# Edge-weight sums of the build: GpSimd compares only, TensorE weighs the hits and keeps a diagonal

## What is computed

```python
src, dst, edge_weight1      # 200000 edges, sorted by dst
h = relu(layernorm(x)); x = x + agg(h)                       # layer 0: degree-normed sums over edges
h = relu(layernorm(x)); x = x + gat2(h)                      # layer 1: two attention layers
h = relu(layernorm(x)); x = x + gat(h)                       # layer 2: attention
h = relu(layernorm(x)); x = x + message_mlp(h, edge_weight1) # layer 3

def _mp_layer(x, src, dst, edge_attr, W, b):                 # twice in layer 3
    msg = concat([x[dst], x[src], edge_attr], 1) @ W + b
    return relu(segment_sum(msg, dst, n))
```

## Time and profile before

| | us |
|---|---|
| runs (3) | 3001.86, 3004.49, 3005.86 |
| median | 3004.49 |
| profiled execution, span | 2998.9 |
| DVE busy in the span | 2360.0 (79%) |
| PE busy | 2558.4 (85%) |
| ACT busy | 1602.9 (53%) |
| POOL busy | 564.6 (19%) |

### The profile page before, as it was taken

One profiled execution on the slowest core, in us unless ns is written; L12 is line 12 of the kernel. 1 busy time (PEld: TensorE's weight loads), 2 busy tenths in 40 slices (PEclk: granted clock), 3 DMA queues, 4 the chain that ended last, 5 costly groups with the idle time before them and its releaser, 6 DMA issues. The chain is left out here.

```text
span 2998.9 us, 77361 instructions
## 1 busy us (share of the span) xinstructions
PE 2558.4 (85%) x25762; PEld 2119.5 (71%) x25763; DVE 2360.0 (79%) x5456; ACT 1602.9 (53%) x2016; POOL 564.6 (19%) x1356
## 2 busy tenths in 40 slices
PE   3648998999899968999878888759999967999998
PEld 2635555555555548999857687639999957888997
DVE  8979999999999976666699999979999995222212
ACT  6023444344444439999898788659888841000101
POOL 0007666676666600000000000000000000000000
PEclk9879999999999988999989899879999978999999
DMA  3003443343344245676536555415545616888998
GB/s 101 0 1 94 113 114 81 99 130 89 81 118 120 80 162 173 221 252 220 188 109 215 171 171 173 149 65 173 185 164 188 214 64 236 293 291 299 322 365 300
DMA packets 448144, 493.82 MB, mean 165 GB/s; under 512 B 132101, under 2 KB 447465, under 8 KB 447850
## 3 DMA queue, kind: packets, MB, share of 16 engines
q1 hardware_dynamic: 300920, 409.16, 40.9%
q10 hardware_dynamic: 147060, 82.71, 9.4%
HBM read 402.61 MB, written 89.17 MB: 164 GB/s over the span
## 5 line engine op out<-in xcount | busy, mean ns | idle before, releaser
L2595 PE MATMUL psum<-sb_arena 128*128 128x198 bf16 (+2 forms) x14406 | 1115.8, 239 | 150.6 <-DVE sb_arena L1883 90.6
L2595 PEld LDWEIGHTS psum<-sb_arena 128*128 128x128 f16 x14406 | 1048.1, 99 | 218.1 <-DVE sb_arena L1883 138.5
L3212 ACT ACTIVATE sb_arena<-sb_arena 128x896 f16 (+1 forms) x1029 | 1014.8, 1047 | 159.1 <-PE psum L2595 123.8
L1877 DVE TENSOR_TENSOR sb_arena<-sb_arena 128x896 f16<-128x896 f16 x1029 | 635.1, 621 | 140.1 <-ACT sb_arena L3212 118.4
L1176 DVE TENSOR_SCALAR sb_arena<-sb_arena 128x392 f16<-128x392 f16 x2352 | 664.6, 348 | 0.0
L2874 ACT ACTIVATE sb_arena<-psum 128x784 f16<-128x784 f32 x392 | 323.2, 824 | 469.1 <-PE psum L2243 404.0
L2243 PE MATMUL psum<-sb_arena 128*128 128x392 f16 x2352 | 479.4, 340 | 79.0 <-DVE sb_arena L1176 65.4
L2243 PEld LDWEIGHTS psum<-sb_arena 128*128 128x128 bf16 x2352 | 280.2, 128 | 257.3 <-DVE sb_arena L1176 103.4
L2660 PE MATMUL psum<-sb_arena 128*128 128x192 bf16 x4802 | 413.8, 247 | 28.9 <-DVEq L2008 16.1
L2660 PEld LDWEIGHTS psum<-sb_arena 128*128 128x128 f16 x4802 | 402.5, 98 | 39.2 <-DVEq L2008 16.9
L1883 DVE TENSOR_TENSOR sb_arena<-sb_arena 128x896 f16<-128x896 f16 x686 | 423.1, 617 | 0.0
(11 more groups left out here) (380 smaller groups left out, 1468.7 us busy)
## 6 DMA issues: line engine op xcount, KB each, us to landing
sb_arena<-counts SPq DMA_DIRECT2D x245, 896.0 KB, 6.6
sb_arena<-counts SPq DMA_DIRECT2D x245, 672.0 KB, 4.7
counts<-sb_arena ACTq DMA_DIRECT2D x56, 1344.0 KB, 5.6
sb_arena<-records SPq DMA_DIRECT2D x392, 6.0 KB, 1.7
sb_arena<-records ACTq DMA_DIRECT2D x392, 6.0 KB, 1.7
counts<-sb_arena SPq DMA_DIRECT2D x1, 5488.0 KB, 19.0
records<-sb_arena SPq DMA_DIRECT2D x1, 3124.0 KB, 8.9
counts<-sb_arena ACTq DMA_DIRECT2D x14, 112.0 KB, 1.7
```

The source lines that it names most:

```text
L1877: nc.vector.tensor_tensor(above_at[r % RING], above_at[r % RING], counts_of(g, j), ALU.mult).then_inc(above_ready, 1)
L2595: last = nc.tensor.matmul(psum[:, bank, at:at + wide], of[:, b * BLK:(b + 1) * BLK], moves[side][:, r, :], start=(r == 0 and at == 0), sto ...
L3212: nc.scalar.activation(above_at[r % RING], of, ACT.Sigmoid, bias=steep_s[:, r:r + 1], scale=STEEP).then_inc(signs_ready, 1)
```

## The change

GpSimd keeps the subtraction and the comparison of each group of four windows; its multiplication and its two additions go. The hits go into one of four buffers (HITS = 4), ordered by tile, so that the 64 hits of one tile lie together. TensorE takes them as weights, with eight moving columns: the edge weights of the group's eight half windows in that tile. Three such matmuls, one for each tile, accumulate a block of 64 rows and 8 columns, of which only the diagonal in steps of 8 rows is wanted. PSUM keeps 56 columns for a chunk instead of 7, ScalarE copies 56, and VectorE masks them at the end with `ea_own`, which it makes once, and adds up each 8.

The matmuls come at the end of the group's last window, behind the pairs, and wait for that group's own hits, no longer for those of the group before. ScalarE's copy moves from window 3 to window 0 of the even half, ahead of the copies of layer 0's sums. `LEA` becomes a buffer of its own, and the buffers behind `ea_hit` lie 640 bytes further on.

```diff
+        def edge_hits_of(i):
+
+            hit = ea_hit[:, i % HITS, :].rearrange("p (t k d) -> p t k d", t=ST, d=SUB)
+            at = at_dst.rearrange("p w (g d) -> p (w g) d", d=SUB).unsqueeze(1).broadcast_to([BLK, ST, 2 * EG, SUB])
+            dst_rel = rel[:, i * EG:(i + 1) * EG, :].rearrange("p w (g t c) -> p t (w g) c", t=ST, c=3)[:, :, :, 1]
+            return hit, at, dst_rel.unsqueeze(3).broadcast_to([BLK, ST, 2 * EG, SUB])
+
...
-                nc.gpsimd.iota(at_dst[:], [[0, 2 * ST], [1, SUB]], base=0, channel_multiplier=0, allow_small_or_imprecise_dtypes=True)
-                pool.drain()
-                nc.gpsimd.tensor_scalar(at_dst[:, ST:2 * ST, :], at_dst[:, ST:2 * ST, :], float(SUB), None, ALU.add)
-                nc.gpsimd.memset(ea_win[:, WH // EG - 1, :], 0.0)
+                nc.gpsimd.iota(at_dst[:], [[0, EG], [1, WIN]], base=0, channel_multiplier=0, allow_small_or_imprecise_dtypes=True)
+                for p0 in (0, EG * WIN):
+                    pool.drain()
+                    nc.gpsimd.iota(ea_past[p0:p0 + EG * WIN, :], [[-SUB, 2 * EG]], base=0, channel_multiplier=1, allow_small_or_imprecise_dtypes=True)
                 pool.drain().then_inc(ea_ready, 1)
                 pool.sem_inc(rel_ready, WS)
...
-                        edge_sums(h, k // EG)
-
-                def edge_sums(h, i):
-
-                    n = WH // EG
-                    wins = rel[:, i % n * EG:(i % n + 1) * EG, :].rearrange("p w (t c) -> p w t c", c=3)
-                    hit = ea_hit.rearrange("p (w t) d -> p w t d", w=EG)
-                    thirds = ea_hit.rearrange("p (w t) d -> p w t d", t=ST)
-                    to = ea_win[:, i % n, :].rearrange("p (w d) -> p w d", d=SUB)
+                        edge_hits(h, k % WH // EG, k // WH)
+
+                def edge_hits(h, i, later):
+
+                    hit, at, dst_rel = edge_hits_of(i)
                     pool.drain()
-                    pool.wait_ge(ea_used, h * n + (i + 1))
-                    nc.gpsimd.tensor_tensor(hit, at_dst[:].unsqueeze(1).broadcast_to([BLK, EG, 2 * ST, SUB]),
-                                            wins[:, :, :, 1].unsqueeze(3).broadcast_to([BLK, EG, 2 * ST, SUB]), ALU.subtract)
+                    pool.wait_ge(ea_used, h * (WH // EG) + (later * (WH // EG) + i + 1))
+                    nc.gpsimd.tensor_tensor(hit, at, dst_rel, ALU.subtract)
                     pool.drain()
-                    nc.gpsimd.tensor_scalar(ea_hit[:], ea_hit[:], 0.0, None, ALU.is_equal)
-                    pool.drain()
-                    nc.gpsimd.tensor_tensor(hit, hit, wins[:, :, :, 2].unsqueeze(3).broadcast_to([BLK, EG, 2 * ST, SUB]), ALU.mult)
-                    pool.drain()
-                    nc.gpsimd.tensor_tensor(to, thirds[:, :, 0, :], thirds[:, :, 1, :], ALU.add)
-                    pool.drain()
-                    nc.gpsimd.tensor_tensor(to, to, thirds[:, :, 2, :], ALU.add).then_inc(ea_ready, 1)
+                    nc.gpsimd.tensor_scalar(ea_hit[:, i % HITS, :], ea_hit[:, i % HITS, :], 0.0, None, ALU.is_equal).then_inc(ea_ready, 1)
 
...
+                dve.wait_ge(ea_ready, 1)
+                nc.vector.tensor_scalar(ea_own[:], ea_past[:], 0.0, None, ALU.is_ge)
+                dve.drain()
+                nc.vector.scalar_tensor_tensor(ea_own[:], ea_past[:], float(SUB), ea_own[:], ALU.is_lt, ALU.mult)
...
-                nc.vector.tensor_copy(ea_sum[:], LEA[:, CB:(CHUNKS + 1) * CB])
+                nc.vector.tensor_tensor(LEA[:, CB:(CHUNKS + 1) * CB, :], LEA[:, CB:(CHUNKS + 1) * CB, :],
+                                        ea_own[:].unsqueeze(1).broadcast_to([BLK, NB, 2 * EG]), ALU.mult)
+                dve.drain()
+                nc.vector.tensor_reduce(ea_sum[:], LEA[:, CB:(CHUNKS + 1) * CB, :], AX.X, ALU.add)
...
-                pe.sem_inc(ea_used, 6)
+                pe.sem_inc(ea_used, HITS - 1)
...
-                def edge_sum(slot, i):
-
-                    odd, n = 1 - slot, WH // EG
-                    p0 = (odd + i) % 2 * EG * WIN
-                    at = EA_AT + (n * odd + i) // 2 % CB
-                    nc.tensor.matmul(psum[p0:p0 + EG * WIN, 5, at:at + 1], ea_win[:, i % n, :], ones[:, 0:1], start=True, stop=True).then_inc(ea_used, 1)
+                def edge_sum(odd, i, h):
+
+                    g = odd * (WH // EG) + i
+                    p0, at = g % 2 * EG * WIN, g // 2 * 2 * EG
+                    wins = rel[:, i * EG:(i + 1) * EG, :].rearrange("p w (g t c) -> p (w g) t c", t=ST, c=3)
+                    pe.wait_ge(ea_ready, h * (WH // EG) + (i + 2))
+                    for t in range(ST):
+                        last = nc.tensor.matmul(psum[p0:p0 + EG * WIN, 5, at:at + 2 * EG], ea_hit[:, i % HITS, t * EG * WIN:(t + 1) * EG * WIN], wins[:, :, t, 2],
+                                                start=t == 0, stop=t == ST - 1, skip_group_check=True)
+                    last.then_inc(ea_used, 1)
 
                 def behind(slot, k, n, c, h):
 
-                    adds = k % EG == EG - 1 and (k < EG or not isinstance(h, int))
-                    if adds:
-                        pe.wait_ge(ea_ready, h * (WH // EG) + (k // EG + 1))
-                    if adds:
-                        edge_sum(slot, k // EG - 1)
...
                             behind(1 - odd, k, w, c, h)
+                            if k % EG == EG - 1:
+                                edge_sum(odd, k // EG, h)
...
-                    act.wait_ge(ea_used, h * (WH // EG) + 7)
-                    to = LEA[:, bass.ds(c * CB, CB)] if not isinstance(c, int) else LEA[:, c * CB:(c + 1) * CB]
-                    nc.scalar.copy(to, psum[:, 5, EA_AT:EA_AT + CB])
+                    act.wait_ge(ea_used, h * (WH // EG) + (HITS - 1))
+                    to = LEA[:, bass.ds(c * CB, CB), :] if not isinstance(c, int) else LEA[:, c * CB:(c + 1) * CB, :]
+                    nc.scalar.copy(to.rearrange("p b k -> p (b k)"), psum[:, 5, 0:CB * 2 * EG])
...
+                            if odd == 0 and k == 0:
+                                edge_sums_out(c, h)
                             if k == 0:
                                 half_sums(odd, h)
-                            if odd == 0 and k == EG - 1:
-                                edge_sums_out(c, h)
```

23 lines of the change are left out of this document (12 added, 11 removed).

## The result

In the same rounds the changed kernel takes 2975.1 us in the median (2967.1 to 2981.6), the kernel before 3003.2 (2999.6 to 3005.9): the ratio is 0.9906, with an interval of 0.9891 to 0.9922. That is 28.1 us less, where 34.5 were forecast; the time lies 5 us above the forecast of 2970 and within its range. Timed a second time with later experiments, the change had 2976.4 (2966.6 to 2986.1), ratio 0.9909 (0.9889 to 0.9930). Its runs lie further apart than those of before, and that turns out to be a part of the story.

What follows compares the result with a forecast made beforehand. VectorE was taken to bound the kernel. Chunks falling from 117.2 to 112.1 us gain 33, the first half 2.8, less 1.1 at the end: 34.7. 3004.5 less 34.5 gives 2970.0 us, range 2960 to 2990.

Steps and rivals of the forecast that it cites:

- VectorE bounds, and loses to GpSimd: Build windows: VectorE sets the pace, 2.093 us a window over a floor of 1.86, losing 0.93 a group to GpSimd's work.
- The term: VectorE in the build: removing GpSimd's three instructions gives back 0.40 us a group, so 111.6 us a chunk.
- the fit: Least squares of 391 VectorE window distances on GpSimd's time in each line: its three instructions cost 0.41 us a group.
- Two more matmuls at 0.27: TensorE at each group's end: two more matmuls cost 0.27 us, in 12 places a chunk, 3.2 us.
- dear matmuls: Rival: two more matmuls cost 0.45 to 0.6 us and TensorE becomes the bound, 2982 to 2994 us; chance 0.17.
- accumulation that doesn't overlap: Rival: matmuls accumulating into the same columns cost full duration, 0.88 us for two; 3016 us, slower than before; chance 0.05.
- TensorE's sum: TensorE's chunk without waits for VectorE: 108.5 us, plus 3.2 for new matmuls and 0.2 for ScalarE's copy, 111.9.
- the mean of before, 5.4: TensorE's windows 2 and 3 of even halves, at granted clock 0.57: 4.5 to 6.2 us in six halves, put at 5.4.
- the sign that the matmuls cost more: Sign of a wrong forecast: the chunk stays above 114 us with TensorE never waiting for VectorE.
- 0.2 on top of the later engine: Chunk time: engines nearly level at 111.6 and 111.9 us, VectorE leading by four windows at most; 0.2 added, making 112.1.
- No wait for hits, records about even: TensorE never waits for the group's hits, with 3.9 us the smallest lead; VectorE's touching records at window 180 cost 0.
- End of the build, 1.1: Build's end: a copy of 0.19 us becomes a multiplication and a reduction, 1.3 with drains, so 1.1 us more.

Runs made afterwards that it cites:

- the last test: The changed kernel plus 16 matmuls of zeros in window 1 of even halves, each group's three new matmuls issued twice: 2993.3 us, ratio 0.9962.
- the second execution: The changed kernel itself, unaltered, timed and profiled once more: 2976.4 us, ratio 0.9909 to the kernel before.
- the filler: 16 matmuls of zeros in window 1 of even halves: added to the changed kernel 2954.7 us, added to the kernel before 3002.8 us.
- loop written out: ScalarE's loop over the chunks written out: in the changed kernel 2957.0 us, again 2955.9; in the kernel before 3002.6.
- with one matmul: The changed kernel with one of the three new matmuls a group instead of three: 2956.9 us, ratio 0.9850.

## Why the prediction was right, and where not

**VectorE bounds, and loses to GpSimd: right.** The floor of 1.86 is still the floor: 251 of the 391 distances are under 1.9 us in the change, 169 were before, and the mean is 2.01 where 2.00 was forecast. Three windows in a row, of which only the third lies under GpSimd's subtraction at 346.88 and the comparison behind it:

```profile
342.09 0.54 DVE L1174 TENSOR_TENSOR sb_arena<-sb_arena 128x768 bf16<-128x768 bf16 x1
...
343.95 0.54 DVE L1174 TENSOR_TENSOR sb_arena<-sb_arena 128x768 bf16<-128x768 bf16 x1
...
345.81 0.54 DVE L1174 TENSOR_TENSOR sb_arena<-sb_arena 128x768 bf16<-128x768 bf16 x1
...
348.02 0.55 DVE L1174 TENSOR_TENSOR sb_arena<-sb_arena 128x768 bf16<-128x768 bf16 x1
```

1.86, 1.86, 2.21. **The term was too small**: 0.41 by the fit, 0.49 by the run that takes only the three away. The fit had the multiplication right (0.27 and 0.27) and the additions nearly (0.14 and 0.18); the whole came out at more than its parts, which only the profiled executions show. VectorE's chunk is 110.4, not 111.6.

The Trainium skill's rule of the exclusive lock ("SBUF — State Buffer", section "SBUF: two separate sides"), taken by duration, had led to 0.47 for the three, and the total agrees with it better than with my fit. Its split does not: by duration the 0.49 would be 0.18 for the multiplication and 0.31 for the additions, and the runs have 0.27 and 0.18. So here the duration of an instruction doesn't tell what it costs VectorE.

**Two more matmuls at 0.27: right**, to the hundredth, and so it was right to stay near the lower end. The rivals of dear matmuls and of accumulation that doesn't overlap fall with it. The Trainium skill's figure for the gap between matmuls ("TensorE: Matmul & The Clock Gate", section "Back-to-back issue gap"), as an estimate 0.32 for four passes, is one for 128 moving columns; these have 8, and it was 0.05 too high for them; the six passes of the last test took 0.35, 0.058 each.

**TensorE's sum: right in all but the clock.** Of the 111.9 forecast, 5.4 + 0.27 were windows 2 and 3 of the even half; at full clock they are 3.74. That makes 111.9 - 5.67 + 3.74 = 110.0, 0.4 under VectorE's 110.4. So the forecast had 1.9 us a chunk for the clock, and it took between 0 and 5.9. At full clock both engines are level, and the change would have had all its gain. With a fall in both halves it is 110.0 + 2.62 + 3.28 = 115.9, and chunks 3 and 4 have 116.1 and 115.9. **This is the step that failed**: I put the mean of before, 5.4, for the clock, as if it were a constant of the place. It was read from the even halves of a kernel where TensorE had time to spare, and the sum's odd half, read from 636.70, had no fall at all; I took over their number and their place. In the change the clock falls in every half of some chunks, in odd ones too, and in none of others. The mean then came out near my 112.1, at 112.5, because VectorE's term was too small and the clock's varied about what I had put. That two engines would end nearly level was foreseen; that the mean met the forecast is luck, and in the second execution it is 114.1. There five chunks of seven are above 114 with TensorE hardly waiting for VectorE, which I had named as the sign that the matmuls cost more. They didn't: the sign can't tell a dear matmul from a slow clock.

**0.2 on top of the later engine: no such term.** While the clock is up, VectorE is the bound; while it falls, TensorE is.

**No wait for hits, records about even: right.** L2212 has an idle time of 0.0 over 488 instructions. VectorE waits for nobody but TensorE (13.3 of 13.4 us). GpSimd itself waits more for records, and that costs nothing, as the list of waits of the changed kernel says, from 343 to 950 us (us in total, times, longest):

```profile
POOL sb_arena L871 <- DMA sb_arena<-records: 176.4, 85, 5.6
PE psum L2246 <- ACT sb_arena L2841: 19.5, 6, 3.8
DVE sb_arena L1174 <- PE psum L2246: 13.3, 17, 1.8
```

**End of the build, 1.1: right.** The rows that answer to the earlier trace rows:

```profile
1055.16 0.57 DVE L1244 TENSOR_TENSOR sb_LEA<-sb_LEA,sb_arena 128x392 f32<-128x392 f32 x1
1055.80 0.56 DVE L1247 TENSOR_REDUCE sb_ea_sum<-sb_LEA 128x49 f32<-128x392 f32 x1
```

1.20 us from the start of the one to the end of the other, where 0.19 were: 1.0.

**The sum.** Between the first comparison and the last 35.8 us of gain were forecast, and 33.0 came in the profiled execution of the change, 22.0 in its second. (The terms of the forecast add up to 34.7; its time was worked out with 34.5.) The profiled spans differ by 30.5, the medians by 28.1. In terms: VectorE gave 48.0 instead of the 39 that 0.40 a group makes over 98 groups, and 15.0 to 26.0 of it went back to TensorE's clock (with the filler only 0.8), where the forecast had TensorE take 3.

**Open.** Why the clock falls in some chunks and not in others. Idle time ahead of it alone is not the answer: the odd half at 397.67 and the one at 509.26 have the same 0.80 us and the same work, and only the second fell; in even halves 3.65 us at 345.78 went without a fall and 3.81 at 570.58 with one. What the runs show is that the falls in even halves follow the idle time behind window 1 (four or all of the five that begin behind ScalarE's return to its loop's start, never in half 12, which stands outside the loop, and none with filler or loop written out, in either kernel), while those in odd halves don't go with it: three each in the change, with one matmul, with filler and written out, and six in the change's second execution. In the change the falls come in series, one in each of seven halves in one execution and of eight in the other. A fall may so bring the next by making its half longer. But the length of a half alone doesn't do it: in the kernel before all halves up to the last take 58.5 to 59.1 us, and the clock fell in one odd half of seven. No run here changed only the length of a half, and so the cause stays open.

## What to carry to other kernels

Before a saving on the bounding engine is counted in full, sum the next engine at full clock, and then separately with each of its stretches at 1.2 GHz: a fall that was hidden in slack costs all of itself as soon as the slack is gone, and it may come more often than it did. If the two engines end level, look at the idle time that precedes the falls; keeping TensorE busy there with work of no value, or removing the idle time, was worth 20 us here and nothing where it had slack. For interference between GpSimd and VectorE, take the instructions away in a run; the share of busy time had the total right and the parts wrong.

## What the hardware showed that I had not expected

- Which of TensorE's stretches run at 1.2 GHz differs between two executions of one program: chunk 1 took 110.4 in one and 116.0 in the other. A fall of 6.8 us cost an even half 2.62 us, an odd one with its fp32 matmuls 3.28; a half with a fall of 3.4 us took 55.0 to 56.0 us, hardly more than one without.
- Sixteen matmuls of zeros in 3.19 us, at one place in every 110 us, keep the granted clock up in all even halves; in the odd ones it fell three times, for 3.4 us each, where the change had three falls of 6.8 us in one execution and five in the other.
- GpSimd's multiplication of 192 elements (0.53 us) cost VectorE 0.27 us, two additions of 64 elements (0.89 us) 0.18, and the three together 0.49.
- The way back of ScalarE's loop costs 2.2 us of TensorE's two first windows (6.04 against 3.86), and none of the kernel's time while VectorE is the bound.
